# Seven pairs of state products added inside SBUF by accumulating GpSimd transfers, in one Mamba and mixture-of-experts kernel

## The reference

```python
def step(h, t):
    dt_t, B_t, C_t, x_t = t
    dA = jnp.exp(dt_t[..., None] * A)
    h = h * dA + dt_t[..., None] * B_t[:, None, :] * x_t[..., None]
    y = jnp.einsum('bds,bs->bd', h, C_t)
    return (h, y)
```

## Time and profile before

| | us |
|---|---|
| median of 3 runs (lowest to highest) | 1485.02 (1483.88 to 1485.74) |
| the profiled execution, its own time | 1487.32 |
| span of the profiled execution | 1485.4 |
| PE busy | 1271.0 (86%) |
| DVE busy | 1055.6 (71%) |
| ACT busy | 1053.5 (71%) |
| POOL busy | 1026.3 (69%) |

### The profile page before, as it was taken

How to read it: one execution, slowest core, us unless ns; L and a number is a source line. 1 busy time by engine, 2 the same in 40 slices (tenths; PEclk the granted TensorE clock), 3 DMA queues, 4 the chain that set the end, 5 groups by cost and what they waited for, 6 DMA issues and landing times.

```text
span 1485.4 us, 24148 instructions
## 1 busy us (share of the span) xinstructions
PE 1271.0 (86%) x7680; PEld 1082.7 (73%) x7680; DVE 1055.6 (71%) x1925; ACT 1053.5 (71%) x2505; POOL 1026.3 (69%) x618
## 2 busy tenths in 40 slices
PE   4487887989989797998989899898989989898986
PEld 2266776877868686787877778687777878787864
DVE  1176868687786867778686876868787786879621
ACT  3498987869777776877767687677868777877410
POOL 1378896877767777676768767687777768687610
PEclk9688999999999999999999999999999999999997
DMA  2301011111121111112111021102102110112001
GB/s 95 121 23 49 31 47 62 37 50 51 44 72 44 51 37 49 54 44 72 36 60 37 29 72 45 63 25 74 42 29 72 44 64 23 68 40 65 29 29 43
DMA packets 29225, 75.09 MB, mean 51 GB/s; under 512 B 3104, under 2 KB 15776, under 8 KB 26528
## 3 DMA queue, kind: packets, MB, share of 16 engines
q1 hardware_dynamic: 29088, 73.41, 15.0%
HBM read 64.61 MB, written 4.59 MB: 47 GB/s over the span
## 4 chain that ended last, share of the span: by engine, by line
PE 60%; DVE 14%; ACT 11%; issue 6%; POOL 1%; DMA 1%; DVEq 0%; ACTq 0%; POOLq 0%; SPq 0%
PE psx L1066 9%; PE psy L1085 9%; PE psb L954 8%; PE pst L960 7%; PE psb L960 7%; PE pst L954 6%; PE psf L954 4%; DVE h L841 4%; ACT dA L677 3%; DVE nx L909 3%; ACT bxT L665 2%; DVE acc L817 2%; PE psf L1042 2%; PE psf L986 2%; PE psf L993 2%
## 5 line engine op out<-in xcount | busy, mean ns | idle before, releaser
L510 POOL TENSOR_TENSOR hC<-h,bC 128x1024 f32<-128x1024 f32 x256 | 606.7, 2371 | 279.9 <-DVE h L841 232.9
L841 DVE TENSOR_TENSOR_SCAN h<-dA,state,psx 128x256 f32<-128x256 f32 x1024 | 680.3, 726 | 93.0 <-PE psx L1066 83.1
L677 ACT ACTIVATE dA<-dt,neg_a 128x256 f32<-128x256 f32 x1024 | 433.7, 497 | 0.0
L1066 PE MATMUL psx<-ident,bxT 128*128 128x128 f32 x2048 | 312.5, 279 | 81.9 <-DVE h L841 74.1
L1066 PEld LDWEIGHTS psx<-ident,bxT 128*128 128x128 f32 x2048 | 248.4, 145 | 119.8 <-DVE h L841 51.3
L665 ACT ACTIVATE bxT<-uTs,BT 128x512 f32<-128x512 f32 x384 | 253.8, 715 | 88.1 <-PE psx L1066 86.4
L1085 PE MATMUL psy<-ident,hC 128*128 128x128 f32 x2048 | 267.0, 274 | 1.1 <-POOL hC L510 1.1
L1085 PEld LDWEIGHTS psy<-ident,hC 128*128 128x128 f32 x2048 | 234.9, 142 | 5.7 <-POOL hC L510 1.3
L494 POOL TENSOR_TENSOR bxT<-uTs,BT 128x1024 f32<-128x1024 f32 x64 | 121.9, 1904 | 26.2 <-PE psx L1066 26.2
L954 PE MATMUL pst<-eT,w_a_sb 128*128 128x256 f32 x512 | 131.9, 404 | 9.3 <-DVE cbc L924 8.8
L954 PE MATMUL psb<-nT,w_ff_sb 128*128 128x256 f32 x512 | 125.6, 388 | 14.1 <-ACT yg L690 12.7
(11 more groups left out here) (117 smaller groups left out, 1620.8 us busy)
## 6 DMA issues: line engine op xcount, KB each, us to landing
bC<-bc_scratch SPq DMA_DIRECT2D x64, 512.0 KB, 4.0
cbc<-cw_scratch SPq DMA_DIRECT2D x16, 1024.0 KB, 4.7
xf<-in_x SPq DMA_DIRECT2D x16, 256.0 KB, 4.1
xk<-xn SPq DMA_DIRECT2D x16, 256.0 KB, 4.3
xb<-in_x SPq DMA_DIRECT2D x16, 256.0 KB, 4.3
out<-x SPq DMA_DIRECT2D x16, 256.0 KB, 2.3
w_in_sb<-in_w_in SPq DMA_DIRECT2D x1, 1024.0 KB, 5.3
w_ff_sb<-in_w_ff SPq DMA_DIRECT2D x1, 1024.0 KB, 5.9
```

The costliest lines, as they stand in the source:

```text
L510: nc.gpsimd.tensor_tensor(hC[:, s % RC], h[:, ring(s)], bC[:, g % RINGG, s % G:s % G + 1, :].to_broadcast([P, NJ, T]), ALU.mult).then_inc( ...
L677: last = nc.scalar.activation(dA[:, s % RA, j, :], dt[:, n[1], j, :], ACT.Exp, scale=neg_a[:, j, s:s + 1])
L841: last = nc.vector.tensor_tensor_scan(h[:, r, j, :], dA[:, s % RA, j, :], psx[bx_bank(fill)][:, k, :], state[:, b, j, s:s + 1], ALU.mult, ...
L1066: last = nc.tensor.transpose(psx[bx_bank(fill)][:, k, j * P:(j + 1) * P], bxT[:, ring(s), j, c:c + P], ident[:, :])
```

## The change

GpSimd, after the product of each odd state below 14, waits for it and issues a transfer from that product's buffer to the buffer of the even state before it, with addition. TensorE waits for that transfer and sums the pair by 8 matmuls from the even buffer; states 14 and 15 are summed singly as before. The pair (s-4, s-3) is summed in part 0 of the even states 4 to 14, the last pair in `back` at state 0, ahead of state 14's sum. The wait of a product for its buffer follows (`summed`).

```diff
+PAIRED = S - 2
+SUMS = PAIRED // 2 + 2
...
+def summed(s):
+
+    return s // 2 + 1 if s < PAIRED else PAIRED // 2 + s - PAIRED + 1
...
+        pair_added = [sem(f"pair_added{k}") for k in range(2)]
...
-                    pool.wait_ge(y_summed, count(S, n, s + 1 - RC))
+                    pool.wait_ge(y_summed, count(SUMS, n, summed(s - RC) if s >= RC else summed(s - RC + S) - SUMS))
                     nc.gpsimd.tensor_tensor(hC[:, s % RC], h[:, ring(s)],
                                             bC[:, g % RINGG, s % G:s % G + 1, :].to_broadcast([P, NJ, T]),
                                             ALU.mult).then_inc(hc_done, 1)
+                    if s % 2 and s < PAIRED:
+                        multiplied = value(count(S, n, s + 1))
+                        pool.wait_ge(ident_ready, 1)
+                        pool.wait_ge(hc_done, multiplied)
+                        nc.gpsimd.dma_start(hC[:, (s - 1) % RC], hC[:, s % RC], accum_op=ALU.add
+                                            ).then_inc(pair_added[s // 2 % 2], 16)
...
-                    dve.wait_ge(y_summed, count(S, m, S))
+                    dve.wait_ge(y_summed, count(SUMS, m, SUMS))
...
-                pe.wait_ge(hc_done, count(S, n, s + 1))
+                if s < PAIRED:
+                    pair = s // 2
+                    per_step = (PAIRED // 2 + 1 - pair % 2) // 2
+                    pe.wait_ge(pair_added[pair % 2], count(16 * per_step, n, 16 * (pair // 2 + 1)))
+                else:
+                    pe.wait_ge(hc_done, count(S, n, s + 1))
...
-                if part == 1:
-                    if s == 2:
-                        add_skip(n)
-                    if s >= 2:
-                        sum_states(s - 2, n)
+                if part == 1 and s == 2:
+                    add_skip(n)
+                if part == 0 and s >= 4 and s % 2 == 0:
+                    sum_states(s - 4, n)
 
             def back(s, m):
+                if s == 0:
+                    sum_states(PAIRED - 2, m)
                 if s in (0, 1):
                     sum_states(S - 2 + s, m)
```

## The result

| | before | after |
|---|---|---|
| median of the runs (4 each) | 1485.38 us (1483.88 to 1486.15) | 1515.67 us (1511.45 to 1518.72) |
| ratio, 95% interval | | 1.0209 [1.0178, 1.024] |
| profiled execution, own time and span | 1487.3, 1485.4 us | 1514.09, 1512.3 us |
| mean granted clock of TensorE | 0.949 | 0.936 |

The account below looks back on a forecast made before the run. TensorE was taken to bound states 7 to 15, a latency chain with no engine busy states 15 to 3. Terms -36 + 3 + 13 + 4 = -16 us gave 1471, as median 1469 us; range 1410 to 1535.

Parts of the forecast that it names:

- The sums that go: States 8 to 15, where TensorE sets the pace: three sums fewer, 2.6 us a step over 14 steps, -36 us.
- The issue on GpSimd: Seven issues a step at 1.2 us each, hidden except at state 1, where 11 steps pay: +13 us.
- The sum that comes at state 0: Second sum in `back` at state 0, 0.87 us ahead of transposes: costed at nothing, 12 us if its cover went.
- VectorE's hold: At state 3 a small VectorE instruction takes 4.33 instead of 0.29 us, locked out while GpSimd reads SBUF.
- The pair's sum at state 4: Sum ahead of the projections at a low clock: between 0 and +0.87 us, taken as +0.3 x 11 steps, +3 us.
- The landing: Transfers take 6 us against 8 to 9 us of slack, so land in time; first two steps cost +4 us once.
- VectorE did not slip past GpSimd: Rival at state 3: VectorE finishes before GpSimd's product of state 2 starts, 45 us go, about 1410 us; chance 0.12.
- The landing was late: Rival at the pair's sum: from about 9 us TensorE waits, each us beyond costs 56 us, about 1540; chance 0.17.
- GpSimd came near to being the bound: Rival at states 8 to 11: at 2.4 us an issue GpSimd needs 26.8 us against TensorE's 20, 1531 us; chance 0.12.
- The clock rival: Fewer matmuls in the latency stretches let TensorE's granted clock fall more often: 1477 to 1500 us; chance 0.10.
- "slower" at 0.37: Chance of a slower kernel: 0.29 from the late landing and GpSimd as bound, 0.08 from the others.

Follow-up runs that it names:

- without transfers: The changed kernel issuing no transfers, sums at the same places, the seven odd products a step left out: 1478.48 us, 0.996 of the kernel before.
- issues alone: The kernel before plus seven accumulating half-tile transfers a step into a spare tile nobody reads, TensorE waiting for none: 1504.19 us, 1.0124.

## Why the prediction was wrong

**"The sums that go" was right.** Predicted 3 x 0.87 = 2.6 us a step between states 8 and 15. The means say 2.49; steps without a piece at a low clock at state 8 say 43.78 to 41.16, which is 2.62. The pairs (6, 7), (8, 9) and (10, 11) alone bring it, 29 us in time.

**"The issue on GpSimd" was right in size and place, and partly by luck in its sum.** 1.2 us was taken, 1.22 found; at state 1 +13 us was forecast, 13.3 measured. But a steady step shows 0.6 to 0.9 us of the 1.22, and the rest of the 13.3 lies in steps 12 and 13 and ahead of the first step. The six other issues were taken as hidden, and cost some 6 us.

**The first failed step is "The sum that comes at state 0", costed at nothing.** It looked at what the two sums stand ahead of, and named VectorE's hold as their cover. It did not look at who waits for the buffers that they free. The product of state 0 did, up to 4.9 us, and all that GpSimd does up to its `bxT` at state 3 moves with it, so the cover itself moved. In the odd steps this still cost nothing, as the term had it. It cost in the steps where the loop goes round and TensorE is late: 1.0 us a step on average from state 0 to 5, and 6.8 us of time, less than the 12 us named for a lost cover.

**The second is "The pair's sum at state 4", a term that was mis-sized.** +3 us was taken between 0 and 0.87 a step; 13.1 us were measured, 1.7 us a step in the piece from 5 to 8. The row there reads 1.92 us for the eight matmuls, near the 1.7 that the prediction had thought for transposes at a low clock. It was also right that part of the projections behind would then fall into the full clock: L968 takes 2.79 us where L954 took 3.62, and L974 1.89 where L960 took 2.78. Counted in TensorE's work alone the term held. What the bound left out is who waits for the first projection: the convolution (ScalarE, then VectorE's taps, L831), and behind it the second projection, which writes the same `psf`. In TensorE's timeline, before (first row) it ran on without idling; in after (second row) it waits for VectorE's taps:

```profile
771.27 1.89 PE L954 MATMUL psf<-uT,w_in_sb 128*128 128x256 f32 x8
```
```profile
786.55 2.79 PE L968 MATMUL psf<-uT,w_in_sb 128*128 128x256 f32 x8
...
793.09 1.99 PE L968 MATMUL psf<-uT,w_in_sb 128*128 128x256 f32 x8 [0.93 <-DVE acc L831]
```

VectorE's first tap starts 5.26 us behind the mark of state 5 before, 6.85 in after and 7.20 without transfers (means of steps 2 to 11), so it moved by 1.6 and 1.9 us, and the piece grew by 1.5 and 1.9. In all ten steps of both kernels the second projection waits 0.88 to 0.93 us for the taps; before it waited 0.06 at most. So the sum lay ahead of a chain of three engines. The 13.1 us are more than the 0.65 us a step by which the ten steady steps became shorter without it: the low clock from state 8 on gave most of the 1.7 back, and half of the 13.1 comes from the last steps and the start.

**The third is "The landing", of which "+4 us once" was the cost of the start.** In the ten steady steps TensorE waits for a transfer once, 0.49 us. The landing took 4.5 to 8.9 us, where 6 was taken, and the slack of 8 to 9 us covered it. At the start it did not. TensorE's timeline of after, the first two steps:

```profile
113.16 1.97 PE L1104 MATMUL psy<-ident,hC 128*128 128x128 f32 x8 [3.50 <-DMA hC<-hC]
...
136.37 1.09 PE L1104 MATMUL psy<-ident,hC 128*128 128x128 f32 x8 [1.44 <-DMA hC<-hC]
...
188.48 1.97 PE L1104 MATMUL psy<-ident,hC 128*128 128x128 f32 x8 [3.18 <-DMA hC<-hC]
...
206.55 1.97 PE L1104 MATMUL psy<-ident,hC 128*128 128x128 f32 x8 [3.98 <-DMA hC<-hC]
```

With the shorter ones between them it is 13.1 us in two steps; the last two steps have 4.0 more and two steps between them 0.75, and together that is the 17.8 us of the page. GpSimd is the engine without time there; the stretch of busy times from 100 to 260 of after (width, then us of each engine with TensorE first, and GpSimd's 140.48 fifth):

```profile
100.00:260.00 160.00, 115.31 (x625) 93.94 (x626) 115.69 (x201) 124.93 (x297) 140.48 (x92) 0.84 0.36 83
```

It is busy 88% of the stretch (81% in before, 129.02 us of the same 160), so an issue that is hidden elsewhere can be time here: issues alone made the first two steps 7.8 us longer, and all of the transfers 17.8 (152.6 against 134.8 without them). No experiment took the transfers out of the first two steps alone; this part rests on the profile.

**The sum again, as measured.** From before to no transfers -6.7 us, where the terms give -36 + 6.8 + 13.1 = -16; 4 of the 9 us between are the stretch ahead of the first step, the rest is open. The steady step closes by its pieces: 0.71 and 1.89 us lost, 2.62 gained by the sums and 0.84 by the low clock that no longer comes at state 8, together -0.86. From there to after +37.2: 19.0 for issues, if half-size transfers stand for whole ones, and 18.2 left. TensorE's 17.8 us of waits for transfers are about as much; that they are the same time is argued, not shown.

**The rivals.** VectorE did not slip past GpSimd: the hold is still there.

```profile
776.06 4.83 DVE L920 TENSOR_TENSOR nx<-nx,earlier 128x128 f32<-128x128 f32 x1
```

The landing was late almost only in the first two and the last two steps, 18 us and not 71. GpSimd came near to being the bound only in the start-up. The clock rival had a part: the clock is low for 197 us instead of 152, and for 205 without transfers, so this goes with the places of the sums and not with the transfers. In the steady steps without transfers 1.7 us more of each are at the low clock from state 0 to 5 and as much from 5 to 8, and 1.7 less from 8 on. How much of the two misplaced sums' cost is this was not told apart. The time fell into the stated range and on the side of "slower" at 0.37, by none of the ways that this chance was built of: there was no rival for a buffer that comes free later, nor for a chain of engines behind a projection.

## What to carry to other kernels

When a consumer is moved, list two things: what it now stands ahead of on its engine, with the engines that wait for that work in turn, and who waits for the buffer that it frees. Here the second was missing, and of the first the chain behind the projection. Move work by transfers only in the stretch where the relieved engine sets the pace (three of seven pairs brought all of the gain, 1456 against 1516 us), and look first for an engine that is held by another one, since a wait of 2.2 us on GpSimd bought 4 us a step.

## What was not expected of the hardware

- A transfer that adds, issued by GpSimd, takes 0.88 us of GpSimd in its row and 1.22 us with the wait for its product. The 512 KB tile lands 4.5 us after the issue when alone, but 7.5 to 8.9 us beside SP's loads of x and `bC`; 256 KB lands in 3.3 us at best. The second 256 KB thus take 1.2 us, some 218 GB/s (an estimate from these two). By the fit of the Trainium skill (DMA: Bandwidth & Descriptors, Anatomy of one DMA) 512 KB would be 3.2 us, an estimate; no run here shows it that short.
- It slows the others' loads as well: `xk` from 4.3 to 5.1 us and `xf` from 4.1 to 5.4 us.
- A VectorE instruction of 0.29 us was held for 4.35 us over two GpSimd instructions that follow each other without a pause.
- To let GpSimd wait on purpose was worth 4.0% of the whole. All seven pairs on top of it lost just that again (1426 to 1485 us), and moving one load of SP that met one transfer gave 34 us back (1451 us).
